# The second mixture of a two-layer decoder: expert tiles scatter their gated rows to a buffer ordered by token, and shared tiles stay on the chip

## The reference

```
scores = sigmoid(X @ gate_w.T)                       # X: 4096 tokens x 256; 32 experts
_, idx = top_k(scores + bias, 4)
w = scores[idx] / sum(scores[idx])
pos = running count of the pairs (token, choice) that chose the same expert
valid = pos < C                                      # C = 256 slots per expert
xe[e, pos] = X[token]                                # only where valid
h = silu(xe @ W1) * (xe @ W3);  ye = h @ W2          # hidden width 128, weights bf16
out = sum over the 4 choices of  where(valid, w, 0) * ye[e, pos]
out = out + silu(X @ sw1.T) * (X @ sw3.T) @ sw2.T    # the shared expert, all tokens
x = layernorm(x + out)                               # what the kernel returns
```

## Time and profile before

| stretch of the span, us | what runs |
|---|---|
| 2320 to 2801 | cross attention of layer two, with router and scatter |
| 2803.4 to 2816.0 | start of the second mixture: first rows and weights |
| 2816.0 to 2910 | the 32 routed tiles |
| 2910 to 2966 | the 16 shared tiles; gathers begin at 2922.0 |
| 2966 to 3162.3 | loads of the shared result, gathers, sums, normalization, output |

### The profile page before, as it was taken

How to read it: one execution, slowest core, us unless ns; L and a number is a source line. 1 busy time by engine, 2 the same in 40 slices (tenths; PEclk the granted TensorE clock), 3 DMA queues, 4 the chain that set the end, 5 groups by cost and what they waited for, 6 DMA issues and landing times. The chain is left out here.

```text
span 3162.3 us, 52554 instructions
## 1 busy us (share of the span) xinstructions
PE 2479.2 (78%) x17441; PEld 2072.9 (66%) x17442; DVE 2038.8 (64%) x5464; ACT 1094.7 (35%) x1952; POOL 886.9 (28%) x1232
## 2 busy tenths in 40 slices
PE   4878787599999699999999999676759899837300
PEld 3666666456665499999999999665636666537300
DVE  5888888366667466666666565565527888736454
ACT  2334343155555322221222222123616555426200
POOL 0000000111111163333332030352112544532674
PEclk8989999699999799999999999888869999869755
DMA  1010001444542210013021110220046665247898
GB/s 54 21 36 20 20 23 57 74 71 72 112 72 45 73 39 29 30 64 106 27 73 66 42 58 27 62 58 18 0 77 98 106 87 84 37 110 217 190 122 86
DMA packets 201931, 210.35 MB, mean 67 GB/s; under 512 B 39890, under 2 KB 188153, under 8 KB 201809
## 3 DMA queue, kind: packets, MB, share of 16 engines
q1 hardware_dynamic: 167936, 145.67, 21.5%
q0 software_dynamic: 18432, 36.94, 7.4%
q10 hardware_dynamic: 15440, 26.22, 2.3%
HBM read 103.42 MB, written 67.90 MB: 54 GB/s over the span
## 5 line engine op out<-in xcount | busy, mean ns | idle before, releaser
L1531 PE MATMUL m_gu<-m_x_hi,m_w_hi 128*128 128x256 f32 x1632 | 462.9, 284 | 17.9 <-issue 10.4
L1531 PE MATMUL m_gu<-m_x_hi,m_w_lo 128*128 128x256 f32 x1632 | 459.1, 281 | 0.0
L1531 PE MATMUL m_gu<-m_x_lo,m_w_hi 128*128 128x256 f32 x1632 | 458.8, 281 | 0.0
L1568 ACT ACTIVATE m_sg<-m_gu 128x256 f32<-128x256 f32 x408 | 156.8, 384 | 670.7 <-PE m_gu L1531 670.7
L1602 DVE TENSOR_TENSOR m_h<-m_sg,m_gu 128x256 f32<-128x256 f32 x408 | 171.6, 421 | 289.2 <-ACT m_sg L1568 286.4
L1067 ACT ACTIVATE x_pt<-x_ps 128x1024 f32<-128x1024 f32 x256 | 262.1, 1024 | 220.9 <-PE x_ps L895 218.6
L1531 PEld LDWEIGHTS m_gu<-m_x_hi,m_w_hi 128*128 128x128 f32 x1632 | 310.3, 190 | 22.2 <-issue 11.8
L1531 PEld LDWEIGHTS m_gu<-m_x_hi,m_w_lo 128*128 128x128 f32 x1632 | 310.3, 190 | 0.0
L1531 PEld LDWEIGHTS m_gu<-m_x_lo,m_w_hi 128*128 128x128 f32 x1632 | 310.2, 190 | 0.0
L1169 DVE CUSTOM_DVE_ANT_0 x_ps<-x_ps,x_mb 128x256 f32<-128x256 f32 x512 | 201.6, 456 | 119.6 <-PE x_ps L895 119.5
L1520 PE MATMUL m_yp<-m_w_hi,m_h_hi 128*128 128x256 f32 x816 | 239.7, 294 | 4.5 <-DVE m_h_lo L1604 4.3
(11 more groups left out here) (303 smaller groups left out, 5846.0 us busy)
## 6 DMA issues: line engine op xcount, KB each, us to landing
m_x<-xs SPq DMA_DIRECT2D x68, 256.0 KB, 3.0
ys<-m_y SPq DMA_DIRECT2D x67, 256.0 KB, 2.2
x_qpack<-x_qh SPq DMA_DIRECT2D x128, 128.0 KB
x_kpack<-x_kh SPq DMA_DIRECT2D x128, 128.0 KB
xs<-zero SPq DMA_DIRECT2D x8, 1024.0 KB, 5.2
x_cx<-in_ctx SPq DMA_DIRECT2D x32, 256.0 KB, 4.5
x_qpack<-x_ql SPq DMA_DIRECT2D x64, 128.0 KB
x_kpack<-x_kl SPq DMA_DIRECT2D x64, 128.0 KB
```

The costliest lines, as they stand in the source:

```text
L1531: ins = pe.matmul(gu[:, m % 4, n, :], wp[n][:, c, m * P:m * P + P], xp_[:, c, :], start=(c == 0 and k == 0), stop=(c == KC - 1 and k == 2))
L1568: act.activation(sg[:, m % 4, :], gu[:, m % 4, 0, :], ACT.Silu).then_inc(silu_ready, 1)
```

## The change

The second mixture is written anew, without loops. What it does:

1. A row of the slot buffer is 12 floats longer (`ROW1` = 268): beside the 256 channels it carries the token's four expert numbers, four values N*K1 - (4*token + j), and its four gates. These lie in `st.rows1`, whose first 256 columns are now `st.res`; the scatter of the attention stage sends all of it. In `place` two small DVE instructions, the mask of the gate and its product, go.
2. Weights are loaded with other DMAs (`load_experts`): rows of 512 bytes for W1 and W3. Those of the first 16 experts and of the shared one are loaded in the middle of the attention stage (six DMAs, `st.w_early`); the other 16 are loaded by three DMAs at the start of the mixture, behind the rows of the first four tiles and ahead of all other rows. To fit, PE reads every second channel for a transpose.
3. Rows are loaded by pair of tiles, three buffers deep, two DMAs per pair; each partition reads two neighbouring rows.
4. For each pair DVE finds, from the expert numbers in the rows, the pair's destination 4*token + j and its gate (`find`, four small instructions). An unfilled slot gets the destination 16384, outside of the buffer, and is dropped.
5. `h` is no longer split: `down` is 2 full-precision matrix multiplications in place of 4 rounded ones. ACT multiplies by the gate while copying to `y` (two instructions of 256 columns instead of one of 512), and POOL scatters the tile's rows to the buffer `yt` of 16384 rows (two indirect DMAs per tile, 64 in all). `y` has four buffers; ACT waits for the scatters of the tile four before.
6. Shared tiles read their rows from `st.res` and add their result to it (`add_shared`); nothing of them goes to DRAM: `xsh`, `ysh` and their loads and stores are gone.
7. For each output block SP loads `yt` with one DMA of 1 MB; the first waits for the last scatters. DVE adds the four parts in two steps, adds them to `st.res`, and normalizes in place. The 128 gathers, the copies of slot numbers and the 128 multiply-and-adds are gone.
8. `yt` is filled with zeros in the RWKV stage: eight DMAs of 2 MB beside the eight of 1 MB.

The diff, cut to its core:

```
+def load_experts(eng, d, dst, first, n, loaded):
+    for k, name in enumerate(("L1_ffn_W1", "L1_ffn_W3")):
+        eng.dma_start(dst[:, 0:n, k * D:k * D + D],
+                      d[name][bass.ds(first, n)].rearrange("e (p k) i -> p e (k i)", k=KC)).then_inc(loaded, 16)
+    eng.dma_start(dst[:, 0:n, 2 * D:3 * D], d["L1_ffn_W2"][bass.ds(first, n)].rearrange("e p c -> p e c")).then_inc(loaded, 16)
...
 # rwkv_stage, sync
                 zero_rows(st.xs1, share * i, share)
+                zero_rows(st.yt, share_y * i, share_y)
...
 # xattn_stage, sync, in the middle period
-                    at(p - 3, store)
+                if not masked and p == B // 2:
+                    load_experts(sp, d, st.w_early, 0, EARLY1, st.early_loaded)
+                    load_experts(sp, d, st.w_early[:, EARLY1:, :], E1, 1, st.early_loaded)
...
 # moe1_stage, sync
+            load_rows(0)
+            load_rows(1)
+            load_experts(sp, d, w_late, EARLY1, LATE, w_loaded)
+            for q in range(2, PAIRS):
+                load_rows(q)
+            for r in range(E1 - YB, E1):
+                until_sent(sp, r)
+            for s in range(B):
+                if s >= W:
+                    sp.wait_ge(summed, s - W + 1)
+                sp.dma_start(yr[:, s % W], yt_v[:, blocks(s)]).then_inc(yr_loaded[s % W], 16)
...
 # gpsimd
+            def send(r):
+                pool.wait_ge(dest_ready, r // 2 + 1)
+                pool.wait_ge(y_ready, r + 1)
                 for t in range(TB):
+                    n = TB * (r % 2) + t
+                    pool.indirect_dma_start(
+                        out=st.yt, out_offset=bass.IndirectOffsetOnAxis(ap=dest[:, r // 2 % DP, n:n + 1], axis=0),
+                        in_=y[:, r % YB, t, :], in_offset=None, bounds_check=N * K1 - 1,
+                        oob_is_err=False).then_inc(y_sent[r % YB], 16)
+            for r in range(E1):
+                if r + U < E1:
+                    widen(r + U)
+                send(r)
...
 # scalar
+            def output(n):
+                r = ORDER[n]
+                act.wait_ge(down_done, n + 1)
+                act.wait_ge(dest_ready, r // 2 + 1)
+                if r >= YB:
+                    until_sent(act, r - YB)
+                for t in range(TB):
+                    k = TB * (r % 2) + t
+                    ins = act.activation(y[:, r % YB, t, :], bank(DOWN + n % U)[:, t, :], ACT.Copy,
+                                         scale=spot[:, r // 2 % DP, k, 1:2])
...
 # vector
+            def add_shared(n):
+                i = SHARED_OF[n]
+                dve.wait_ge(down_done, n + 1)
+                dve.tensor_tensor(st.res[:, blocks(i), :], st.res[:, blocks(i), :], bank(DOWN + n % U), ALU.add).then_inc(added, 1)
...
+            def sum_up(i):
+                u = i % W
+                dve.wait_ge(yr_loaded[u], 16 * (i // W + 1))
+                s.do(dve.tensor_tensor(yr[:, u, :, 0:2, :], yr[:, u, :, 0:2, :], yr[:, u, :, 2:4, :], ALU.add))
+                s.do(dve.tensor_tensor(yr[:, u, :, 0, :], yr[:, u, :, 0, :], yr[:, u, :, 1, :], ALU.add))
+                n_sum = s.mark(dve.tensor_tensor(st.res[:, blocks(i), :], st.res[:, blocks(i), :], yr[:, u, :, 0, :], ALU.add))
```

More of the change, by code:

```diff
@@ L2125, in _ @@
-            gate_up(0, 0)
-            with pe.Fori(0, pairs - 1) as i:
-                turn(i + 1, 0)
-                gate_up(i, 1)
-                down(i, 0)
-                turn(i + 1, 1)
-                gate_up(i + 1, 0)
-                down(i, 1)
-            gate_up(pairs - 1, 1)
-            for u in range(U):
-                down(pairs - 1, u)
+            for n in range(-2, TILES):
+                if n + 2 < TILES:
+                    turn(n + 2)
+                if 0 <= n + 1 < TILES:
+                    gate_up(n + 1)
+                if n >= 0:
+                    down(n)
@@ L2187, in _, with high @@
[L2187 to L2194 removed]
+            def high(n):
+                act.wait_ge(t_ready, n + 1)
+                if n >= U:
+                    act.wait_ge(gu_ready, n - U + 1)
+                act.activation(x_hi[:, n % U], bank(TURN + n % U), ACT.Copy).then_inc(xh_ready, 1)
@@ new lines, in widen_down @@
+            def widen_down(r):
+                if r == EARLY1:
+                    act.wait_ge(w_loaded, 16 * 3)
+                if r >= U:
+                    act.wait_ge(down_done, TILE_OF[r - U] + 1)
+                act.activation(w2[:, r % U], expert(r)[:, 2 * D:3 * D], ACT.Copy).then_inc(w2_ready, 1)
+            act.activation(w2s[:], st.w_early[:, EARLY1, 2 * D:3 * D], ACT.Copy).then_inc(w2s_ready, 1)
+            for r in range(U):
+                widen_down(r)
+            for n in range(-2, TILES):
+                if n + 2 < TILES:
+                    high(n + 2)
+                if 0 <= n + 1 < TILES:
+                    gate(n + 1)
+                if n >= 0 and ORDER[n] is not None:
+                    output(n)
+                    if ORDER[n] + U < E1:
+                        widen_down(ORDER[n] + U)
@@ L2234, in normalize @@
[L2234 to L2245 removed]
+            s = Chain(dve, steps)
@@ new lines, in normalize @@
+            def normalize(i):
+                dve.wait_ge(rstdr, i + 1)
+                dve_normalize(dve, st.res[:, blocks(i), :], st.res[:, blocks(i), :], var, rstd, i % W).then_inc(xn_ready, 1)
+            for n in range(-2, TILES):
+                if n + 2 < TILES:
+                    low(n + 2)
+                if 0 <= n + 1 < TILES:
+                    hidden(n + 1)
+                if n >= 0 and ORDER[n] is None:
+                    add_shared(n)
+                if n + 1 < TILES and ORDER[n + 1] is not None and ORDER[n + 1] % 2 == 0:
+                    find(ORDER[n + 1] // 2)
@@ L2248, in xattn0_stage @@
+            for i in range(B):
+                sum_up(i)
+                if i:
+                    normalize(i - 1)
+            normalize(B - 1)
 def xattn0_stage(nc, st, d):
```

429 lines of the change are left out of this document (155 added, 274 removed).

## The result

Four runs of the changed kernel took 3036.16 to 3049.96 us, median 3041.78; the kernel before, beside them and earlier, 3162.23 (3159.88 to 3170.22). The ratio is 0.9617, 95% interval 0.9588 to 0.9646: **faster by 3.8%**. The forecast was 3033 us, range 3012 to 3080. The profiled execution took 3040.17 us, span 3038.5, mean granted clock 0.909.

The account below looks back on a forecast made before the run. POOL was to pace the routed tiles, PE the shared ones, DVE the output: 2950.8 + 73.6 - 0.6 + 6.9 = 3030.7, plus 2.5 for late weights and one instruction, 3033 us; range 3012 to 3080.

Parts of the forecast that it names:

- The main term, POOL's pace: Routed tiles: POOL's widening (0.75 us) and two scatters (2.55) make 3.4 us per tile with semaphores, setting the pace.
- `down` at 0.50, "no change": PE per tile: two full-precision multiplications take 0.50 us, about as four rounded ones, so a tile stays at 2.1 us.
- The start: Start of the second mixture, set at 2803.4: rows land by 2806.30, first multiplication at 2809.0 instead of 2816.0.
- Late weights: Routed tiles: 3.1 MB of weights ahead of tile 4's rows take 9 us, perhaps 16; cost +2 us.
- rival 5: Start of the mixture: late weights hold the rows of tile 4 until 2834; +12 us, 3045; chance 0.09.
- The transposes: PE's transposes reading every second channel cost 0, at most 0.46 us per shared tile, 7 us.
- The output: Last part: DVE takes 4.6 us per block without waiting for loads, 16 blocks 73.6 us, then 6.9 from last aggregate to end.
- 1 (clock low all stage): Routed and shared tiles: PE's gaps of 1.3 us lower the clock, tiles take 3.8 us; +40, 3073; chance 0.10.
- 2 (send at 1.69): Routed tiles: each POOL scatter costs 1.69 us instead of 0.97, pace 4.8; +45, 3078; chance 0.07.
- 3 (output bound by DMA): Output: 21 MB at 118 GB/s take 178 us from 2921, ending at 3108; chance 0.05.
- 4 (waits for landings): Routed tiles: ACT and DVE wait for scatters of four tiles before; at 35 us landing +179, 3212; chance 0.03.
- may be why they are slow: Kernel before, output gathers: four in five reading the same spare rows was offered as a possible cause of the DMA engines' slowness.

Follow-up runs that it names:

- experiment 4: Changed kernel with h split again by DVE and `down` as 4 rounded multiplications: mixture 249.8 us against 255.8, ratio to the kernel before 0.9539.
- experiment 3: Changed kernel with the three late weight DMAs issued behind the rows of tiles 4 and 5: mixture 252.4 us against 255.8, ratio to the kernel before 0.9623.
- experiment 2: Changed kernel with tiles ordered two routed, one shared: mixture 227.4 us against 255.8; separately, with one send per routed tile instead of two: 233.9 us.
- experiment 1: Kernel before, with invalid pairs pointed at 128 different spare rows instead of one: mixture 345.4 us against 381.5, ratio 0.9932.

## Why the prediction was right, step by step

**The main term, POOL's pace.** Right: 3.37 us against 3.4, and one send less takes 22 us off. Its parts: the widening of 512 columns is 0.62, inside the bounds (0.75 taken); a send is 0.98, and 0.30 lies between the two. That the sum came out so close is luck in part: a tile in which POOL waits only 0.2 takes 3.08 (2850.57 to 2853.65). The other 0.29 are half of the longer wait for `y` in every second tile, which the sum did not have; the widening and the gap behind the second send, both taken too long, made up for it. 0.19 of that wait go when `down` is shorter (experiment 4).

**`down` at 0.50, "no change".** Wrong by its size: 0.87 against 0.48. The row, `x8` in 2.00 us, was read as eight multiplications; it is four, since a full-precision one is listed twice (2 in the code stand as `x4` after). The other half of the step was wrong as well: the 2.09 us of the earlier trace rows were not free of waiting. In the trace of the kernel before, the `down` between them begins here:

```profile
2908.27 0.28 PE L2119 MATMUL m_ps<-m_w,m_h_hi 128*128 128x256 f32 x1
```

It is done 0.48 later, and the next tile begins at 2908.91, so 0.16 was empty. Of the 0.39 more that `down` takes, only 0.17 therefore shows: shared tiles are 2.27 instead of 2.1, +2.7 us over 16.

**The start.** The stage began 1.9 us later than set (2805.39 against 2803.49 for SP's first transfer). Zeros, early weights and wider rows lie ahead of it, counted 0, but the parts ahead of the mixture vary by up to 20 us between profiles, so the cause isn't shown. The first multiplication was 0.5 later again, which is the term of +0.5 for one more instruction at the start. **Late weights** were taken at +2 and cost more: a wait of 5.74 us at tile 4, of which experiment 3 gave back 3.4. The "perhaps 16" us for them had no row behind it; they took SP 6.9 us to issue and landed 9.9 us after issue in the median. This is rival 5 in its mechanism, at about a third of its 12. **The transposes**, which read every second channel now, are no slower: 0.63 us for four in the shared tiles against 0.66, so 0 was right.

**The output.** Right: no wait for `yt`, first addition 1.22 (1.24 taken), blocks 4.50 (4.6), aggregate to end 3038.5 - 3031.6 = 6.9. From the first sum to the end 77.9 against 79.9.

**The ledger.** First sum forecast 2950.8 + 2.5 = 2953.3, seen 2960.6: +1.9 attention, +2.7 `down`; the 2.7 left are tile 4 beyond its +2, less what the pace gave back (an estimate, not taken apart further). Output -2.0. So +5.3 on 3033: 3038.5.

**The rivals.** 1 (clock low all stage): refuted, granted clock 1.00 from 2840 to 2958, in spite of a wait in every routed tile. A long wait does lower it: behind the 5.74 us four transposes take 1.13 us instead of 0.63. The rule of the Trainium skill (TensorE: Matmul & The Clock Gate, second failure mode) does not show at gaps of 0.6 to 1.2 us. 2 (send at 1.69): refuted, 0.967 to 0.988 over all 64. 3 (output bound by DMA): refuted; eight blocks lie ready, and in experiment 2 the loads of 1 MB moved 413 GB/s from 2940 to 2962. The 118 GB/s before were not the DMA engines' limit: with the spare rows spread the rate from 2985 to 3120 is 123 GB/s at a DMA share of 0.41, against 110 at 0.89 before, since POOL's issues set the pace in both (experiment 1). The one row made the engines busy, not the rate low; "may be why they are slow" holds for the landing. 4 (waits for landings): refuted by eight buffers.

**What the prediction missed** is not in its number. It said that PE would wait in each routed tile and that the shared tiles would follow at PE's pace, but did not add that the two could overlap; that was worth 28 us by length, 18 by the ratio.

## What to carry to other kernels

When one engine must issue something for every tile of one kind, put tiles that need nothing of it between them: here that took 28 us off the mixture without changing an instruction. Look at which addresses an indirect transfer reads, too: padding that all points to one row cost 36 us of the mixture's length, 22 of the kernel's time, and spreading it over 128 rows is a small edit. And before a busy share is called a limit, look at who issues the work: DMA engines 90% occupied were not what set the pace of a block. Check how often the list shows an instruction for each one in the code before taking a price from a count.

## What the runs showed of the hardware

- Indirect gathers of 1 KB rows of which most read one same row (four in five, an estimate) occupy the DMA engines 0.736 x 177 / 11.54 = 11.3 us per MB, and 0.265 x 146 / 11.15 = 3.5 us per MB when the spare reads go to 128 rows.
- Two full-precision multiplications of 128x256 take 0.87 us, four rounded ones 0.48.
- POOL's tiny instructions stretch beside DVE's additions. Timeline of the version with the normalization on ACT:

```profile
2973.24 1.19 DVE L2180 TENSOR_TENSOR m_yr<-m_yr 128x1024 f32<-128x1024 f32 x1
2973.40 1.08 POOL L2020 TENSOR_TENSOR m_rstd<-m_var,eps 128x2 f32<-128x2 f32 x1 [0.99 <-DVE m_var L201]
```

  Two numbers per partition take 1.08 us, and end with the addition. In the kernel before the same instruction took 0.20 at 3041.99, where DVE had just ended its last sum (3041.94) and began its statistics, which have one input. The Trainium skill (SBUF — State Buffer, two separate sides) says that a DVE instruction with two SBUF inputs holds a port that POOL needs to read, for its whole length. These rows agree. It cost nothing here: POOL's four instructions fit into the 3.85 us of a block, and DVE did not wait.
- DVE widens 128x512 from bf16 in 0.42 us, POOL in 0.62, ACT in 0.65.
- Four and more indirect DMAs issued back to back, 1.28 us apart, went with waits of ACT of 2 to 3.4 us; at the gap shown, nothing that ACT waits for by the program was late in the trace. Neither the place of the copy nor the number of buffers changed that; a short POOL instruction between did. The cause is open.
